# Chosen experts, second attention and routed experts in one block with landing waits; constants made in the first attention; paddings on two queues

## What is computed

```python
h = tok(x, patch_size=16)                      # linear map of 768 pixels to 128, plus bias
h = h + attn0(layernorm(h))                    # one causal head; inputs and weights rounded to few levels
h = h + ffn0(layernorm(h))
h = h + attn1(layernorm(h))                    # 8 causal heads of 16, layernorm on q and k
h = h + ffn1(layernorm(h))

def ffn0(x):                                   # chosen experts: each of 8 experts picks 1024 tokens
    probs = softmax(x @ Wr, axis=0)            # over the tokens
    vals, idx = top_k(probs.T, 1024)
    h = gelu(x[idx] @ W1 + b1)                 # 128 -> 512
    y = h @ W2 + b2                            # 512 -> 128
    return zeros.at[idx].add(vals * y)

def ffn1(x):                                   # routed experts: each token picks 2 of 8 experts
    w, idx = top_k(x @ Wg + bg, 2); w = softmax(w)
    h = silu(x @ W1[e] + b1[e]);  y = h @ W2[e] + b2[e]
    return sum of w * y over the two experts
```

## Time and profile before

| | |
|---|---|
| runs | 2004.06, 2000.64, 2002.51 us; median 2002.51 us |
| the profiled execution | 2003.38 us |
| its span in the profile | 2001.70 us |
| TensorE clock, mean granted | 0.92 of full speed |
| PE busy | 1703.6 us, 85% |
| DVE busy | 1224.1 us, 61% |
| POOL busy | 1138.6 us, 57% |
| ACT busy | 1071.5 us, 54% |

### The profile page before, as it was taken

One profiled execution on the slowest core, in us unless ns is written; L12 is line 12 of the kernel. 1 busy time (PEld: TensorE's weight loads), 2 busy tenths in 40 slices (PEclk: granted clock), 3 DMA queues, 4 the chain that ended last, 5 costly groups with the idle time before them and its releaser, 6 DMA issues. The chain is left out here.

```text
span 2001.7 us, 44426 instructions
## 1 busy us (share of the span) xinstructions
PE 1703.6 (85%) x13083; PEld 1263.3 (63%) x13084; DVE 1224.1 (61%) x4791; ACT 1071.5 (54%) x2510; POOL 1138.6 (57%) x1037
## 2 busy tenths in 40 slices
PE   4999999984448874599999999999982899998996
PEld 2566655653426653266766767667662798998985
DVE  2889988873741000589999999999965222322221
ACT  2666666652415442366666676666741455555553
POOL 2444444432245885125666666666656487877776
PEclk8999999996559887699999999999996899999998
DMA  8988899931013342201111121111112576776774
GB/s 202 208 218 210 213 212 215 217 87 57 0 36 52 66 64 35 78 26 48 46 50 52 47 54 47 50 54 44 44 39 68 116 137 125 137 134 121 136 133 79
DMA packets 270771, 198.08 MB, mean 99 GB/s; under 512 B 25326, under 2 KB 251152, under 8 KB 270608
## 3 DMA queue, kind: packets, MB, share of 16 engines
q1 hardware_dynamic: 220624, 160.65, 32.0%
q0 software_dynamic: 49984, 35.38, 13.0%
HBM read 143.33 MB, written 52.40 MB: 98 GB/s over the span
## 5 line engine op out<-in xcount | busy, mean ns | idle before, releaser
L2271 POOL DMA_INDIRECT out_dram<-r_yw,r_idx x212 | 328.4, 1549 | 121.4 <-issue 61.0
L2143 POOL DMA_INDIRECT rows_scratch<-routed_row,slot_u x256 | 252.5, 986 | 205.9 <-DVE slot_u L2094 142.0
L1817 ACT ACTIVATE a_probsT<-a_p_sc 98x392 f32<-98x392 f32 x384 | 173.5, 503 | 151.2 <-PE a_p_sc L1598 96.0
L2339 ACT ACTIVATE r_hT<-r_p_up,r_b1T 128x256 f32<-128x256 f32 x424 | 191.5, 473 | 113.4 <-PE r_p_up L2313 81.2
L2300 PEld LDWEIGHTS r_p_y<-w_all,r_hT 128*128 128x128 f32 x1696 | 223.1, 192 | 11.1
L2300 PE MATMUL r_p_y<-w_all,r_hT 128*128 x1696 | 223.6, 275 | 0.0
L2313 PE MATMUL r_p_up<-r_xgT,r_w1e 128*128 128x256 f32 x848 | 221.5, 385 | 0.6 <-ACT r_xgT L2344 0.6
L415 PE MATMUL p_embed<-pix,w_pix 96*128 96x392 f32 x512 | 208.1, 513 | 3.5 <-ACT pix L530 3.5
L680 POOL TENSOR_SCALAR vare<-mv 98x4 f32<-98x4 f32 x64 | 30.4, 476 | 229.5 <-DVE mv L665 195.4
L1914 DVE TENSOR_REDUCE a_negmax<-a_p_max 98x2 bf16<-98x392 f32 x256 | 132.1, 556 | 44.9 <-PE a_p_max L1565 40.6
L2356 DVE TENSOR_TENSOR r_yb<-r_p_y,b_all 128x256 f32<-128x256 f32 x106 | 45.0, 425 | 186.1 <-PE r_p_y L2300 156.3
(11 more groups left out here) (367 smaller groups left out, 4125.8 us busy)
## 6 DMA issues: line engine op xcount, KB each, us to landing
img<-in_x_dram SPq DMA_DIRECT2D x192, 196.0 KB, 4.2
img<-in_x_dram SPq DMA_DIRECT2D x192, 189.0 KB, 4.4
r_w1e<-in_L_ffn_W_dram SPq DMA_DIRECT2D x106, 256.0 KB
r_xg<-rows_scratch SPq DMA_DIRECT2D x106, 130.0 KB
xn_scratch<-xn SPq DMA_DIRECT2D x32, 196.0 KB
h_scratch<-h SPq DMA_DIRECT2D x32, 196.0 KB
h<-h_scratch SPq DMA_DIRECT2D x32, 196.0 KB
h3b<-h_scratch SPq DMA_DIRECT2D x32, 196.0 KB
```

The costliest lines, as they stand in the source:

```text
L1817: act.activation(probsT[:, u % 2, i, :], p_sc[i % 2][:, 0:2 * PAIR], ACT.Exp).then_inc(exped, 1)
L2143: pool.indirect_dma_start(rows_dram, bass.IndirectOffsetOnAxis(ap=slot_u[:, u % ROWS, c, t:t + 1], axis=0), row[:, u % ROWS, c, t, :], Non ...
L2271: pool.indirect_dma_start(acc_dram, bass.IndirectOffsetOnAxis(ap=idx[:, (k - 3) % 4, t:t + 1], axis=0), yw[:, (k - 3) % 4, t, :], None, co ...
L2339: act.activation(hT[:, (k - 1) % 2, f, :], p_up[f][:, 0:G], ACT.Silu, bias=b1T[:, bass.ds(e * FC + f, 1)]).then_inc(act_h, 1)
```

## The change

1. The last three stages are one block. `topk_experts`, `attend_and_route` and `routed_experts` no longer open blocks but return their five lists and a function of waits; `stages` calls them one after the other for each engine. Between chosen experts and second attention each engine waits itself for the four `added` semaphores (`all_added`); between second attention and routed experts each waits for the h stores, the scatters, the tables and the paddings (`all_routed`). The block of the first attention keeps its end.
2. The constants for the later stages are made by POOL in the first attention. `made.make` is cut in three: the fills and index patterns when the pixels of unit 8 are prepared, the 98x4096 clear of `vals` in four parts at units 10 to 13 (`clear_vals`), the selects at unit 16 (`select`), and `groups.constants` at unit 18. In each case they stand behind POOL's two pixel copies.
3. The paddings are shared out. The two fixed ones are issued by SP at the start of the second attention (`pad_behind`), ahead of its first load; the eight regions are padded behind the second attention, experts 0 to 3 by SP and 4 to 7 by ACT.
4. DVE's `mark_past` for experts 1 and 2 stands behind the hits of expert 0, and those of the later experts behind the hits of the expert two before; it was one expert ahead, and before the hits.
5. ACT weighs group 13 before it forms the last expert's weights (`chances(7)`); before, it came behind the steps of that turn.

```diff
 embed_and_attend(nc, sb, ps, sem, early, made, groups, x, ...)
-topk_experts(...); attend_and_route(...); routed_experts(...)      # a block each
+chosen = topk_experts(...)
+second = attend_and_route(...)
+routed = routed_experts(...)
+def stages(eng, i):
+    chosen[i](eng)
+    chosen[-1](eng)
+    second[i](eng)
+    second[-1](eng)
+    routed[i](eng)
...
@@ first attention, POOL, behind the pixel copies of a unit
+                if ahead == 8:
+                    made.make(pool)
+                if 10 <= ahead < 10 + made.VALS:
+                    made.clear_vals(pool, ahead - 10)
+                if ahead == 16:
+                    made.select(pool)
+                if ahead == 18:
+                    groups.constants(pool)
...
@@ chosen experts, POOL
                 pool.tensor_scalar(low[:], prob[:].bitcast(U16)[:, 0::2], -32768.0, None, ALU.add
                                    ).then_inc(tc, 1)
-                made.make(pool)
-                groups.constants(pool)
...
-                for r in range(RINGY):
-                    pool.wait_ge(added[r], 16 * GT * len(range(r, GROUPS, RINGY)))
+        def all_added(eng):
+            for r in range(RINGY):
+                eng.wait_ge(added[r], 16 * GT * len(range(r, GROUPS, RINGY)))
...
@@ chosen experts, ACT
                 for n in range(GROUPS + 3):
                     if live(n, 3, GROUPS):
                         weigh(n - 3)
+                    if n == GROUPS:
+                        chances(EXPERTS - 1)
                     for f in range(FC):
...
-                    if n < GROUPS and n % PG == PG - 1:
-                        ... exponent of expert n // PG
+                    if n < GROUPS - 1 and n % PG == PG - 1:
+                        chances(n // PG)
...
@@ chosen experts, DVE
                 mark_past(0)
                 for e in range(EXPERTS):
-                    if e + 1 < EXPERTS:
-                        mark_past(e + 1)
                     for i in (2 * e, 2 * e + 1):
                         ... hits and tok_u of piece i
+                    for ahead in (1, 2) if e == 0 else (e + 2,):
+                        if ahead < EXPERTS:
+                            mark_past(ahead)
...
@@ constants
+    def clear_vals(self, pool, i):
+        pool.memset(self.vals[:, i], 0.0).then_inc(self.cst, 1)
...
-        for t in (aux_l, aux_r, vals):
+        for t in (aux_l, aux_r):
             pool.memset(t[:], 0.0).then_inc(cst, 1)
...
-        pool.wait_ge(cst, 10)
+    def select(self, pool):
+        pool.wait_ge(cst, 9 + self.VALS)
...
@@ paddings
+    def wait(self, eng):
+        eng.wait_ge(self.tabs, self.TABLES)
+        eng.wait_ge(self.padded, 16 * (EXPERTS + 2))
-    def pad_regions(self, sp):
-        sp.wait_ge(self.tabs, 1)
+    def pad_behind(self, sp):
         sp.wait_ge(self.cst, 8)
-        for e in range(EXPERTS):
-            ... the region of expert e
         ... the two fixed ones
-        sp.wait_ge(self.padded, 16 * (EXPERTS + 2))
+    def pad_regions(self, eng, experts):
+        eng.wait_ge(self.tabs, 1)
+        for e in experts:
+            ... the region of expert e
...
@@ second attention
+            groups.pad_behind(sp)
             straight(sp, emit, DEPTH, UNITS)
-            groups.pad_regions(sp)
-            for s in h4_stored:
-                sp.wait_ge(s, 16 * UNITS // 2)
+            groups.pad_regions(sp, range(0, EXPERTS // 2))
...
             straight(act, emit, DEPTH, UNITS)
+            groups.pad_regions(act, range(EXPERTS // 2, EXPERTS))
...
-            for i, s in enumerate(scattered):
-                pool.wait_ge(s, 16 * 2 * TPU * len(range(i, UNITS, ROWS)))
+        def all_routed(eng):
+            for s in h4_stored:
+                eng.wait_ge(s, 16 * UNITS // 2)
+            for i, s in enumerate(scattered):
+                eng.wait_ge(s, 16 * 2 * TPU * len(range(i, UNITS, ROWS)))
+            groups.wait(eng)
```

931 lines of the change are left out of this document (464 added, 467 removed).

## The result

Over 15 runs each the changed kernel has a median of 1995.97 us and the kernel before 2002.83 us; the ratio is 0.9958 (95% interval 0.9948 to 0.9967), that is 8.4 us saved (6.6 to 10.4). Forecast were 15.3 us. The time lies at the very upper edge of the stated range (1981 to 1996 us), in the part that was added to the forecast's own ends (1983 to 1993) for two rivals that did not come about: that it lies inside is partly luck.

A forecast was written before the change was run, and what follows sets the result against it. No engine bounds the whole, the prediction said: four chained stages lose time at seams and in a serial search. Gains 4.3 + 6.7 + 3.9 + 3.4 + 0.5 = 18.8 us, less 3.5 paid: 15.3 us, median 1987.2 us, range 1981 to 1996.

The forecast's parts named there:

- First seam: Between chosen experts and second attention: removing barrier and drain, less the paddings' cost, gains 4.3 us (3.6 to 5.0).
- the drain returns: Rival at the first seam: POOL's settling delays the next stage's first instruction, costing 5.6 us, 1992.8 us; chance 0.06.
- Second seam: Between second attention and routed experts: waits replace the barrier, paddings are shared by SP and ACT; gains 6.7 us (3.8 to 6.7).
- the 2.4 us of reserve: Second seam: the paddings, landed by 1542.9 us, could take 2.4 us more before showing behind POOL's scatters at 1545.3.
- Search: Head of the chosen experts: constants leave the 20-step search, its one long step of 6.04 us becomes 2.18; gains 3.9 us.
- First attention: Where the constants move to: they delay DVE and POOL there, costing 3.5 us (bounds 0 and 16.4).
- the moved work is paid in full: Rival in the first attention: every moved POOL instruction blocks DVE, costing 16.4 us instead of 3.5, 2000.1 us; chance 0.08.
- a worse rhythm: Slower case in the first attention: 24 units each pay 1.3 us, 31 us, giving 2014.7 us; chance 0.03.
- First tokens: Start of the chosen experts' gathers: hits directly follow PE's look-up, the first gather comes 3.4 us sooner (0 to 3.4).
- hidden: Rival on the early tokens: something else holds the experts' start, 11.9 us gained in all, 1990.6 us; chance 0.10.
- Last chances: End of the chosen experts: ACT weighs group 13 before the last exponent, POOL's scatter 0.5 us sooner (-0.5 to 0.5).
- some 9 us paid: Upper end of the forecast's own range, 1993 us: the moved constants cost some 9 us in the first attention.

The follow-up runs named there:

- best: Changed kernel with constants at the first attention's end, last 8 of 24 gathers held, fixed paddings behind the second attention's eighth unit: 0.9910 of the kernel before.
- tail: Changed kernel with the constants made at the end of the first attention, behind POOL's last pixel copies: 0.9926 of the kernel before.
- search: Changed kernel with the constants back in the search, the clear of vals still in four parts: 0.9945 of the kernel before.
- oldlook: Changed kernel with the old look-up order, the later expert's mark_past ahead of the first hits: 0.9965 of the kernel before.
- again: Changed kernel run once more without any edit, on the first chip of the experiments: 0.9941 of the kernel before.
- after: First profiled execution of the changed kernel, 1999.22 us, the slowest of its 15 runs; their median was 1995.97 us.
- third: Changed kernel run a third time without any edit, on the third chip: 0.9949 of the kernel before.
- onepad: Changed kernel with all eight region paddings issued by SP, none by ACT: 0.9959 of the kernel before.
- before: First profiled execution of the kernel before, without the change: 2003.38 us.
- moved: Kernel before with only the constants moved into the first attention, at units 8, 10 to 13, 16 and 18: 1.0009 of the kernel before.

## Why the prediction was right, and where its sum was too large

**First seam, 4.3 us forecast.** 3.6 to 4.0 us in all pairs of traces. Drain gone, paddings paid; their delay in transit was nearer to the upper end of my 0 to 1.4 us, as `best` shows with 1.9 us for both together (issue 1.0, transit 0.9). The rival "the drain returns" is out: no stall follows. Its reason, that the drain grows with what was issued, does not hold either: the drain of 5.6 us stood behind 128 indirect DMAs of POOL, that of 2.7 us behind 256.

**Second seam, 6.7 us forecast.** 6.65 us, so the number was right, but two of its steps were not. Paddings on two queues are not as fast as on one, 2.7 to 3.9 us each on SP instead of 2.2 (1.5 to 2.4 on ACT), and the 2.4 us of reserve that I gave them were used up in `tail` and `search` (load 6.65 and 5.42 us behind the scatter instead of some 4). And 6.7 us is what a chip gives on which a padding takes 2.2 us; where it takes 1.1, 2.95 us.

**Search, 3.9 us forecast.** 3.83 us. The cause that I named (POOL's memsets hold DVE) is right; that the constants have to leave for it is not: three quarters of it come from cutting the memset in four. The selects do hold DVE, 0.5 us at a time, and the small operation at 505.60 could not show it: the two selects of `aux_l` stand apart, and the first had only 0.11 us left, less than the 0.16 us that the operation takes by itself.

```profile
504.82 0.90 POOL L1234 TENSOR_SCALAR_AFFINE_SELECT aux_l<-aux_l 128x784 bf16<-128x784 bf16 x1
```

The Trainium skill's rule (SBUF — State Buffer, Who interferes with whom), a hold for the whole length of the instruction that issued first, agrees with these rows, selects included, better than my reading of one row did. A hold through several memsets, as that of 4.74 us, goes beyond it.

**First attention, 3.5 us forecast.** 3.0 us by the means of six and eight traces (give or take 2.4; 3.6 us when counted from unit 8 on), 0 to 7 in single ones, and 6.6 at the head of the search in the profiled execution. So neither the rival that the moved work is paid in full (16.4 us) nor that of a worse rhythm (31 us) came about. The 1 us each for units 8 and 16 is what the traces show where PE's clock stays up (0.7 to 1.1 and 0.8 to 1.0 us). The 1.2 us for the parts of `vals` were too many (0.05), and PE's clock, which adds 2 to 3 us at the fills in two of six traces and at the selects in three, was in no term. The two errors partly cancel in the mean: that the sum came out is in part luck.

**First tokens, 3.4 us forecast.** 3.68 us at the gather, by `oldlook` against `again` 3.4 at the experts' first exponent and 2.9 at the last scatter. The rival "hidden" is out.

**Last chances, 0.5 us.** The last scatter of group 13 (of 0 to 15) stands 159.01 us behind the first of all in the kernel before and 158.56 in `again`: 0.45 us. Right there, but the first of group 14 stands 163.18 and 162.92 us behind it: 0.26 us are left, and they reach the end.

**Sum.** Working with the stretches of the traces on chips like the first, the change gives 3.8 + 3.7 + 3.7 + 6.6 = 17.8 us at the four places, pays 3.0 in the first attention, and loses 1.5 between first gather and last scatter (230.5 us in the mean of `after`, `again`, `third`, `onepad`, two of them with the stretches at the lower clock described below; 229.0 in `before` and `moved`) and 1.1 in the routed experts (440.4 against 439.3). That is 12.2 us, and measured were 8.4 (6.6 to 10.4), 11.9 (8.2 to 15.5) and 10.2 (7.0 to 13.4). The step that failed is the last sentence of the sum: "All stages behind a gain are themselves chains, which start sooner as a whole". They start sooner, but they do not all last equally long: in `after` and `third` POOL's scatters of the chosen experts take 2.5 us more than in `again`, 1.4 us at the second group, of which 0.6 come back later, and 1.7 at group 14. What the runs show in its place is again PE's clock, a term that the sum does not have. `after` and `third`, and none of the other seven traces with 24 gathers in a row on such chips, have a stretch at the lower clock 51 us behind the first gather and another at 211.5 us, ahead of these two scatters. At group 14, `again`, then `after`; the window starts 1.5 us ahead of the matmul row in both:

```profile
761.65:765.25 3.60, 3.41 (x20) 2.32 (x18) 0.15 (x1) 1.54 (x3) 3.11 (x2) 1.00 0.40 36
...
763.15 1.02 PE L993 MATMUL p_up<-xgT,w1e 128*128 128x512 f32 x2
```

```profile
770.20:773.80 3.60, 3.60 (x13) 2.57 (x12) 0.00 (x0) 0.84 (x2) 2.50 (x2) 0.53 0.38 32
...
771.70 1.91 PE L993 MATMUL p_up<-xgT,w1e 128*128 128x512 f32 x2
```

These stretches stand in two of seven traces with the changed experts on such chips (`after`, `again`, `third`, `onepad`, `tail`, `search`, `oldlook`) and in neither of two with the old ones (`before`, `moved`); `again` has the same code as `after` and `third` and does not have them, and whether they belong to the change, so few traces cannot tell. The distance from 12.2 us to the 8.4 of the longest measurement also stays open.

The range had a fault of its own: no term gives the "some 9 us paid" at its end of 1993 us; with the first attention's upper bound, 16.4 us, that end would be at 2000 us.

## What to carry to other kernels

Price a seam by what each engine waits for last, and check that price where transfers are slow and where they are fast: the same barrier was worth 6.6 us on one chip and 3.0 on another, since another queue stood behind it. Before work is moved out of a serial chain, look whether it can be cut there: four short memsets took 2.9 of the 3.9 us out of the search, and moving all constants on gave the last 0.9 us and cost 3.0 in the place where they went. And put moved work where its neighbours idle (behind a pipeline's last units, as in `tail`, whose trace has no price for it), not where only its own engine does. Where a pause of PE can follow, price its clock too, and do it from several traces: with one and the same code it fell in some executions and not in others.

## What the runs showed of the hardware

- An engine that runs beside a row of POOL's indirect DMAs can be late by itself: on the first and third chip, with 24 gathers in a row, ACT answered up to 8.4 us late although what it waited for was done (`oldlook`; 7.7 us in the row of `before` above), and its first exponent came 5.3 to 6.1 us behind the last gather, whenever that was. On the second chip, with the same code, it was not late (15 us sooner). Breaking the run after 16 brought 6 us at the exponent and 3 at the last scatter (one trace). What holds ACT, no trace shows.
- The same two kinds of chip differ in the issue of a padding by SP beside POOL's scatters: 2.2 us and 1.1 us each. On the slower kind a second queue slowed the first, to 2.7 to 3.9 us; on the faster it did not (four in 4.43 us). Whether both come from one cause wasn't tried.
- A POOL memset or select holds a small DVE operation until it ends, and a row of memsets can hold it through several: 4.74 us through three, 3.84 us (2.4 of them fills) through a copy and seven. With the longest one cut in four, DVE was let in behind the second part, and no part made a step of the search longer.
- In a full pipeline such a hold let PE pause. Its granted clock fell behind that pause in two of six traces at the fills and in three of six at the selects, and the price rose from some 1 us to 2.6 to 4.3.
- Executions differ by some 4 us in where the first attention's last copies stand (414.3 to 418.0 us in eight traces with nothing moved in front of them; 416.1 to 423.6 in three of the changed kernel), so one trace of each kernel can't price a change in such a stage.
